# A rank-one memory layer in blocks of 32: block rows in a factored form, and their products placed behind the next block's pivots

## Chip, cores and metric

One Trainium2 chip (trn2), one core. The metric is the device time of one execution in microseconds (us), for the whole program.

## What is computed

A decoder of four layers over 64 sequences of 128 tokens with 128 channels. The change concerns the first operation of layer 0, a memory with a recursive least-squares state per sequence:

```
Q, K, V = x Wq + bq, x Wk + bk, x Wv + bv        # (64, 128, 128) each
A = eye(128); M = 0                              # per sequence
for t in range(128):
    s = sum(k * q)
    u = k / (norm(k) + 1e-6)
    Au = A @ u
    denom = 1 + sum(u * Au)
    A = A - outer(Au, Au) / denom
    z = Au / denom
    M = M + outer(v, s * z)
    o = M @ q
out = O @ Wo + bo
```

All vectors z (128 per sequence) and the dots s are computed first, by a memory phase; the decoder that follows (attention, experts and norms of all four layers) reads them from DRAM.

## The kernel before

The program has two parts, one behind the other: `memory_phase` and `decoder_phase`. All data is fp32. Each engine runs its own program; programs of several "threads" are merged by a string per engine in `MEMORY_ORDER`, one character for each step (up to a `yield`), executed in that order whatever is ready. A digit is a thread, w is the work that all share. SyncE issues all DMAs.

The memory phase handles 64 sequences as 16 quads of four; quad q belongs to thread q mod 4 (`THREADS = 4`), and each thread owns two PSUM banks, `Yb` and `Tb`. Stages:

- **Keys** (first loop of each `memory_quads_*`): TensorE projects queries and keys of a quad (L743), VectorE adds the bias (L839, L842), forms k times q (L848) and its sum, the dot s (L852), k times k (L855) and its sum (L859), GpSimd takes the root (L910), VectorE adds eps (L863), inverts (L867) and scales, giving u (L873). TensorE transposes u (L749), ScalarE evacuates it to `uT` (L807).
- **Block rows** for each block of 32 tokens (`BLK`, four blocks): for each quad y = U A, in both orientations (L765, L768), copied by ScalarE (L816) and VectorE (L881), then the Gram matrix g = y U^T of 32x32 per sequence (L775), copied to `g` (L886).
- **Trip of the small matrices**: SyncE stores g to DRAM (L995) and loads it with one sequence per partition into `E`, 64x32x64 (L999). VectorE adds 1 to the diagonal (L946) and does 31 pivots of an elimination, four instructions each (L953 to L963), for all sequences at once; then it writes the inverse factor and the same scaled by the inverse pivots into `xx` (L971, L974). SyncE stores xx (L1002) and loads it in eight DMAs as block-diagonal stationary operands `xs`, 128x128 for each quad (L1011).
- **Solve and update**: TensorE multiplies y by both factors (L791, L792) and gets the block's z (L793, copied by ScalarE over the keys in `uT`, L821). In the first three blocks, ScalarE copies W (L826), VectorE spreads the scaled product over four sequences with a mask (L894), one matmul of 512 columns forms the update (L798), and VectorE subtracts it from `A`, 128x128 for each sequence (L899). The next block's rows need the updated A.
- **End**: s and z are stored to DRAM (L1017, L1021), and the decoder's setup begins.

What sets the order around the change is thus a circle in each block: rows and Gram need A, the trip needs all 16 quads of g, the solve needs the trip, A needs the solve.

## Time and profile before

| | us |
|---|---|
| median of 3 runs | 6566.8 (6562.96 to 6573.8) |
| the profiled execution, its own time | 6575.45 |
| its span in the trace | 6573.4 |
| memory phase, to the end of the store of z | 655.72 |
| decoder with its setup | 5917.68 |

The trace is of one execution. Its stages are told apart by the DMAs of SyncE. PE is TensorE's matmuls, PEld its weight loads, DVE is VectorE, ACT ScalarE, POOL GpSimd, SPq SyncE's queue. One fp32 matmul of the program appears as two instructions. PEclk is the granted clock as a share of 2.4 GHz.

### The profile page before, as it was taken

What the parts mean: (1) busy time and instruction counts of PE and PEld (TensorE: products, weight loads), DVE (VectorE), ACT (ScalarE), POOL (GpSimd) and SP (SyncE); (2) the same over time, 40 slices, a digit from 0 to 9 for tenths busy, and PEclk for the clock granted to TensorE, in tenths of its full rate; (3) what the DMA queues carried; (4) which work ended last, traced back from release to release, by engine and by line L of the source; (5) the groups of instructions that cost most, each with busy time, mean ns of one, the idle gap of its engine ahead of it and who ended that gap; (6) DMA issues with size and microseconds to landing.
All of it is one profiled execution on the core that took longest, in us unless ns stands there. A gap on an engine that the chain in (4) does not pass through costs nothing.

```text
span 6573.4 us, 128828 instructions
## 1 busy us (share of the span) xinstructions
PE 5160.7 (79%) x54833; PEld 3769.1 (57%) x54833; DVE 3783.7 (58%) x9917; ACT 2358.7 (36%) x4452; POOL 512.8 (8%) x470
## 2 busy tenths in 40 slices
PE   5334477789897778888888888888778889878878
PEld 4223366556666556666656655666555566655656
DVE  6665256665555665655565565565655554566554
ACT  1000133443424344433443443433443433433442
POOL 1000100001100000100000001000100110000010
PEclk6666597999998989999888999999998989888989
DMA  1001210000021000001001001101000011100001
GB/s 31 10 17 38 75 52 27 1 1 27 21 80 38 16 1 17 28 28 56 27 27 34 27 2 34 38 23 52 9 27 16 20 36 50 38 16 16 14 1 49
DMA packets 144922, 184.39 MB, mean 28 GB/s; under 512 B 46202, under 2 KB 73826, under 8 KB 143714
## 3 DMA queue, kind: packets, MB, share of 16 engines
q1 hardware_dynamic: 144354, 176.17, 8.7%
q8 instruction: 436, 7.14, 0.5%
q14 instruction: 132, 1.08, 0.1%
HBM read 164.25 MB, written 11.57 MB: 27 GB/s over the span
## 4 chain that ended last, share of the span: by engine, by line
PE 59%; DVE 15%; ACT 8%; issue 5%; POOL 1%; DMA 1%; SPq 0%; POOLq 0%; DVEq 0%; ACTq 0%
PE g_bank L2515 7%; PE g_bank L2500 7%; PE g_bank L1426 5%; PE g_bank L1448 5%; PE g_bank L1398 5%; ACT g_keys_exps L1478 5%; DVE g_tops L1491 4%; PE g_bank L1459 2%; PE g_bank L1369 2%; PE g_bank L1773 2%; PE g_bank L1307 1%; PE g_bank L1787 1%; PE g_bank L2246 1%; PE g_bank L1411 1%; PE g_bank L2108 1%
## 5 line engine op out<-in xcount | busy, mean ns | idle before, releaser
L1491 DVE TENSOR_REDUCE g_tops<-g_bank 128x4 f32<-128x308 f32 (+1 forms) x1536 | 812.0, 574 | 535.6 <-PE g_bank L1398 532.4
L1478 ACT ACTIVATE g_keys_exps<-g_bank 77x512 f32<-77x512 f32 (+1 forms) x1536 | 802.5, 596 | 731.6 <-PE g_bank L1426 730.9
L1242 POOL TENSOR_TENSOR g_rstd<-g_rstd,minus_half 128x4 f32<-128x4 f32 x224 | 231.5, 1034 | 4560.8 <-DVE g_rstd L1225 4555.3
L1426 PE MATMUL g_bank<-g_qa,g_keys_exps 32*77 32x128 f32 (+1 forms) x12288 | 489.1, 302 | 112.5 <-DVE g_o L1511 59.8
L1426 PEld LDWEIGHTS g_bank<-g_qa,g_keys_exps 32*77 32x77 f32 (+1 forms) x12288 | 409.3, 183 | 227.9 <-DVE g_o L1511 83.5
L1398 PE MATMUL g_bank<-g_keys_exps,g_qa 32*128 32x154 f32 (+1 forms) x6144 | 415.4, 388 | 145.7 <-ACT g_keys_exps L1478 107.6
L1448 PE MATMUL g_bank<-g_keys_exps,g_v 77*32 77x128 f32 (+1 forms) x12288 | 455.8, 294 | 87.9 <-DVE g_tops L1491 74.9
L2515 PEld LDWEIGHTS g_bank<-L_places,g_keys_exps 128*128 128x128 f32 x4096 | 472.7, 192 | 51.7 <-issue 49.9
L2500 PE MATMUL g_bank<-g_xT,L_places 128*128 128x512 f32 x1024 | 496.0, 615 | 2.6 <-DMA L_places<-L_w_in 2.6
L2515 PE MATMUL g_bank<-L_places,g_keys_exps 128*128 128x128 f32 x4096 | 481.6, 276 | 7.8 <-DVE g_base L2545 7.7
L1448 PEld LDWEIGHTS g_bank<-g_keys_exps,g_v 77*32 77x32 f32 (+1 forms) x12288 | 343.1, 117 | 201.9 <-DVE g_tops L1491 146.9
L1472 ACT ACTIVATE g_oT_sc<-g_bank 128x512 f32<-128x512 f32 x384 | 228.5, 598 | 603.7 <-PE g_bank L1448 603.2
L1398 PEld LDWEIGHTS g_bank<-g_keys_exps,g_qa 32*128 32x128 f32 x6144 | 278.2, 203 | 260.0 <-ACT g_keys_exps L1478 146.5
L2526 ACT ACTIVATE g_keys_exps<-g_bank,weights_sb 128x512 f32<-128x512 f32 x256 | 175.6, 686 | 490.8 <-PE g_bank L2500 490.5
L2545 DVE SCALAR_TENSOR_TENSOR g_base<-g_bank,g_gates,g_base 128x128 f32<-128x128 f32 x512 | 152.6, 342 | 286.4 <-PE g_bank L2515 286.3
L1459 PE MATMUL g_bank<-consts_sb,g_oT_sc 128*128 128x128 f32 x1536 | 260.5, 295 | 52.7 <-ACT g_keys_exps L1478 25.2
L1494 DVE TENSOR_TENSOR g_qa<-g_qa,g_bank 128x256 f32<-128x256 f32 x384 | 159.7, 416 | 231.7 <-PE g_bank L1411 230.1
L2500 PEld LDWEIGHTS g_bank<-g_xT,L_places 128*128 128x128 f32 x1024 | 185.7, 196 | 178.0 <-issue 154.5
L791 PE MATMUL m_bank<-m_y,m_xs 128*128 128x128 f32 x128 | 29.4, 316 | 320.8 <-DMA m_xs<-xx_scratch 320.8
L2538 DVE TENSOR_SCALAR g_keys_exps<-g_bank,weights_sb 128x512 f32<-128x512 f32 x256 | 189.2, 745 | 146.2 <-PE g_bank L2500 146.1
L1251 ACT ACTIVATE g_x<-g_x,g_shift,g_rstd 128x128 f32<-128x128 f32 x384 | 176.8, 487 | 229.8 <-DVE g_shift L1228 229.2
L1459 PEld LDWEIGHTS g_bank<-consts_sb,g_oT_sc 128*128 128x128 f32 x1536 | 177.8, 148 | 136.2 <-issue 64.6
(360 smaller groups left out, 9170.3 us busy)
## 6 DMA issues: line engine op xcount, KB each, us to landing
L_places<-L_w_in SPq DMA_DIRECT2D x512, 256.0 KB, 2.8
m_xT<-xT_in SPq DMA_DIRECT2D x16, 256.0 KB, 2.7
z_scratch<-m_uT SPq DMA_DIRECT2D x1, 4096.0 KB, 11.1
g_oT_sc<-z_scratch SPq DMA_DIRECT2D x16, 256.0 KB, 2.9
g_xT<-xT_in SPq DMA_DIRECT2D x16, 256.0 KB, 3.5
g_o<-x_in SPq DMA_DIRECT2D x16, 256.0 KB, 4.0
out<-g_x SPq DMA_DIRECT2D x16, 256.0 KB, 2.3
weights_sb<-weights_in SPq DMA_DIRECT2D x1, 3021.0 KB, 9.9
```

What stands on the lines that cost most here:

```text
L1242: e.tensor_tensor(g.rstd[:, :], g.rstd[:, :], g.s["minus_half"], ALU.pow).then_inc(*b.gpsimd(st + " rstd"))
L1251: e.activation(out[:, n, :], src[:, n, :], ACT.Identity, bias=g.shift[:, n:n + 1], scale=g.rstd[:, n:n + 1]).then_inc(*b.scalar(f"{st} nor ...
L1398: ins = e.matmul(bank[r][:, 2 * nk * t:2 * nk * (t + 1)].rearrange("p (i k) -> p i k", i=2), g.qa[rows, t, n, :], g.km[rows, n, t, :, 0:nk ...
L1426: ins = e.matmul(bank[r][0:nk, u * T:(u + 1) * T], g.km[rows, n, t, i, 0:nk], g.qa[rows, t, n, :], start=not masked, stop=not masked or u ...
L1448: ins = e.matmul(b.bank[st][0][32 * u:32 * u + 32, r * T:(r + 1) * T], g.v[0:nk, n, 4 * r + u, :], g.p[0:nk, r, u, :], start=True, stop=True)
L1459: ins = e.transpose(b.bank[st][1][:, r * P:(r + 1) * P], outputs_of(g, n)[:, r, :], g.k["ident"])
L1472: e.activation(outputs_of(g, n - 1), seqs(bank[0][:, :]), ACT.Copy).then_inc(*b.scalar(f"{st} oT {n - 1}"))
L1478: e.activation(g.p[0:nk, r, :, :], bank[r][0:nk, :].rearrange("p (u q) -> p u q", u=4), ACT.Exp, scale=scale).then_inc(*b.scalar(f"{st} p ...
L1491: e.tensor_reduce(g.tops[:, :, first:first + 2], src, AX, ALU.max).then_inc(*b.vector(f"{st} top {n} {r}"))
L2500: e.matmul(bank[k % 3][:, :], weights.part(f"w1 {x}", c), g.xT, start=True, stop=True).then_inc(*b.tensor(f"f3 hidden {k}"))
L2515: ins = e.matmul(bank[3][:, n * D:(n + 1) * D], g.gated_hid[:, x % 2, c, n * T:(n + 1) * T], weights.part(f"w2 {x}", c), start=c == 0, sto ...
L2538: e.tensor_scalar(g.gated_hid[:, x % 2, k % HC, :], b.bank["ex"][k % 3][:, :], g.w["f3_b1"][:, k:k + 1], 0.0, ALU.add, ALU.max).then_inc(* ...
```

## The change

A is no longer formed or updated. With blocks before it solved, A = I minus a sum of terms, one per block, so a block's rows times the columns that are still needed are: U times [later keys | I], minus V_i times W_i for each earlier block i. `rows` holds for each quad (four sequences, 32 partitions each) those products with the keys of the later blocks (columns up to 128) and with I (128 more). W_i is the factor (now with the sign changed) times rows, V_i the scaled factor times the part over later keys.

- **Keys**: three threads. k times q moves to GpSimd, the squares to ScalarE with accumulation (the second product and the second sum leave VectorE). The first block's Gram matrix is U U^T, four small matmuls a quad into one bank `diag` (bank 6) for all quads, and one copy of 128x512 to g.
- **rest_tensor, rest_scalar**: one block's rows without the diagonal columns, and, for the block before, the remaining columns of W and V and its z. They have no VectorE part.
- **early_diagonal**: the part of the next block's Gram matrix that doesn't need the block's factors, accumulated in `diag`.
- **next_pairs, next_diagonal**: once the factors are loaded, W and V for the next block's 32 columns alone, in four chunks of four quads, and their product, added to `diag`. W is copied by ScalarE, V by VectorE.
- The last block has its solve alone; z is copied by ScalarE and VectorE in four pieces.
- The load of the mask is gone; xx gets the factor multiplied by -1. Elimination, DMAs of g, E, xx and xs are as before, with waits on one semaphore instead of four.

Cut to its core (the order strings, semaphores and the loops of the keys are left out but for what moves between engines):

```diff
-THREADS = 4
+THREADS = 3
...
+def keys_tensor_of(e, me, i):
...
+        e.wait_ge(me.uT_set[i], n + 1)
+        for j in range(4):
+            u = me.uT[:, 4 * q + j, cols_of(0)]
+            ins = e.matmul(me.diag[32 * j:32 * j + 32, q * BLK:(q + 1) * BLK], u, u, start=True, stop=True)
+        ins.then_inc(me.gram[i], 1)
+        yield
+def keys_scalar_of(e, me, i):
...
+            e.activation(me.squares[i][:, b, :], me.qk[i][:, b, D:2 * D], ACT.Square,
+                         accum_out=me.norm[:, 4 * q + b:4 * q + b + 1]).then_inc(me.squared[i], 1)
...
+def keys_gpsimd_of(e, me, i):
...
+        e.tensor_tensor(me.tmp[i][:, :, :], me.qk[i][:, :, D:2 * D], me.qk[i][:, :, 0:D], ALU.mult
+                        ).then_inc(me.multiplied[i], 1)
...
+def rest_tensor(e, me, blk):
+
+    at = (blk + 1) * BLK
+    own = cols_of(blk)
+    for q in range(me.nq):
+        done = blk * me.nq + q
+        W_bank, rows_bank = me.bank[q % 2 * 2], me.bank[q % 2 * 2 + 1]
+        if blk:
+            before = done - me.nq
+            e.wait_ge(me.rows_set, before + 1)
+            if before >= 2:
+                e.wait_ge(me.W_set, before - 1)
+                e.wait_ge(me.z_set, before - 1)
+                e.wait_ge(me.V_set, min(before - 1, (NBLK - 2) * me.nq))
+            x, scaled, rows = me.xs[:, q, 0, :], me.xs[:, q, 1, :], me.rows[:, q, :]
+            e.matmul(W_bank[:, 0:T + D - at], x, rows[:, at:T + D], start=True, stop=True)
+            if at < T:
+                e.matmul(W_bank[:, 256:256 + T - at], scaled, rows[:, at:T], start=True, stop=True)
+            e.matmul(W_bank[:, 384:512], rows[:, T:T + D], scaled, start=True, stop=True).then_inc(me.solved, 1)
+            yield
+            e.wait_ge(me.W_set, before + 1)
+            if at < T:
+                e.wait_ge(me.V_set, before + 1)
+        else:
+            for i in range(THREADS):
+                e.wait_ge(me.uT_set[i], len(quads_of(me, i)))
+        if done >= 2:
+            e.wait_ge(me.rows_set, done - 1)
+        for j in range(4):
+            lane, u = slice(32 * j, 32 * j + 32), me.uT[:, 4 * q + j, :]
+            if at < T:
+                e.matmul(rows_bank[lane, at:T], u[:, own], u[:, at:T], start=True, stop=False)
+            ins = e.matmul(rows_bank[lane, T:T + D], u[:, own], me.ident[:, :], start=at == T, stop=blk == 0)
+        for i in range(blk):
+            for j in range(4):
+                lane = slice(32 * j, 32 * j + 32)
+                ins = e.matmul(rows_bank[lane, at:T + D], me.V[lane, i, q, own.start - BLK:own.stop - BLK],
+                               me.W[lane, i, q, at - BLK:], start=False, stop=i == blk - 1)
+        ins.then_inc(me.rows_ready, 1)
+        yield
+
+def rest_scalar(e, me, blk):
...
+            e.wait_ge(me.solved, before + 1)
+            e.activation(me.W[:, blk - 1, q, at - BLK:], W_bank[:, 0:T + D - at], ACT.Copy).then_inc(me.W_set, 1)
+            yield
+            if at < T:
+                e.wait_ge(me.solved, before + 1)
+                e.activation(me.V[:, blk - 1, q, at - BLK:], W_bank[:, 256:256 + T - at], ACT.Copy).then_inc(me.V_set, 1)
+                yield
+            e.wait_ge(me.solved, before + 1)
+            e.activation(me.uT[:, 4 * q:4 * q + 4, cols_of(blk - 1)], four(W_bank[:, 384:512]), ACT.Copy
+                         ).then_inc(me.z_set, 1)
+            yield
+        e.wait_ge(me.rows_ready, done + 1)
+        e.activation(me.rows[:, q, at:], rows_bank[:, at:T + D], ACT.Copy).then_inc(me.rows_set, 1)
+        yield
...
+def early_diagonal(e, me, blk):
+
+    own = cols_of(blk + 1)
+    e.wait_ge(me.g_set, blk + 1)
+    for q in range(me.nq):
+        at = slice(q * BLK, (q + 1) * BLK)
+        for j in range(4):
+            u = me.uT[:, 4 * q + j, own]
+            e.matmul(me.diag[32 * j:32 * j + 32, at], u, u, start=q == 0, stop=False)
+        for i in range(blk):
+            for j in range(4):
+                lane = slice(32 * j, 32 * j + 32)
+                e.matmul(me.diag[lane, at], me.V[lane, i, q, cols_of(blk)], me.W[lane, i, q, cols_of(blk)],
+                         start=False, stop=False)
+        yield
+
...
+PAIR_BANKS = ((4, 5), (7, 0), (1, 2), (3, 4))
+
+
+def pairs_in(me, c, k):
+    return me.bank[PAIR_BANKS[c][k]][:, 0:4 * BLK].rearrange("p (q m) -> p q m", q=4)
...
+def next_pairs(e, me, blk, c):
+
+    at = (blk + 1) * BLK
+    if c == 1:
+        e.wait_ge(me.rows_set, (blk + 1) * me.nq)
+        if blk:
+            e.wait_ge(me.W_set, blk * me.nq)
+            e.wait_ge(me.V_set, blk * me.nq)
+            e.wait_ge(me.z_set, blk * me.nq)
+    elif c == 3:
+        e.wait_ge(me.next_W, 4 * blk + 1)
+    for q in range(4 * c, 4 * c + 4):
+        e.wait_ge(me.rows_set, blk * me.nq + q + 1)
+        out = slice(q % 4 * BLK, (q % 4 + 1) * BLK)
+        for k in range(2):
+            ins = e.matmul(me.bank[PAIR_BANKS[c][k]][:, out], me.xs[:, q, k, :], me.rows[:, q, at:at + BLK],
+                           start=True, stop=True)
+    ins.then_inc(me.pair_ready, 1)
+    yield
+
+
+def next_diagonal(e, me, blk, c):
+
+    part = cols_of(blk)
+    e.wait_ge(me.next_W, 4 * blk + c + 1)
+    e.wait_ge(me.next_V, 4 * blk + c + 1)
+    for q in range(4 * c, 4 * c + 4):
+        at = slice(q * BLK, (q + 1) * BLK)
+        for j in range(4):
+            lane = slice(32 * j, 32 * j + 32)
+            ins = e.matmul(me.diag[lane, at], me.V[lane, blk, q, part], me.W[lane, blk, q, part], start=False,
+                           stop=q == me.nq - 1)
+    ins.then_inc(me.diag_ready, 1)
+    yield
...
+def memory_tensor(e, me):
+
+    chunks = me.nq // 4
+    for blk in range(NBLK):
+        yield from rest_tensor(e, me, blk)
+        if blk < NBLK - 1:
+            yield from early_diagonal(e, me, blk)
+        e.wait_ge(me.xs_loaded, 128 * (blk + 1))
+        if blk < NBLK - 1:
+            if blk:
+                e.wait_ge(me.next_W, 4 * blk)
+                e.wait_ge(me.next_V, 4 * blk)
+            yield from next_pairs(e, me, blk, 0)
+            for c in range(1, chunks):
+                yield from next_pairs(e, me, blk, c)
+                yield from next_diagonal(e, me, blk, c - 1)
+            yield from next_diagonal(e, me, blk, chunks - 1)
+    for q in range(me.nq):
+        e.wait_ge(me.rows_set, NBLK * me.nq)
+        e.wait_ge(me.W_set, (NBLK - 1) * me.nq)
+        e.wait_ge(me.z_set, (NBLK - 1) * me.nq)
+        e.matmul(me.bank[q // 4][:, (q % 4) * P:(q % 4 + 1) * P], me.rows[:, q, T:T + D], me.xs[:, q, 1, :],
...
@@ memory_vector, in the loop over the blocks, behind the clears of E
+        if blk:
...
+            for c in range(me.nq // 4):
+                e.wait_ge(me.pair_ready, 4 * blk - 4 + c + 1)
+                e.tensor_copy(me.V[:, blk - 1, 4 * c:4 * c + 4, cols_of(blk - 1)], pairs_in(me, c, 1)).then_inc(me.next_V, 1)
+                yield
+            e.wait_ge(me.diag_ready, 4 * blk)
+            e.wait_ge(me.g_stored, 16 * blk)
+        else:
...
+        e.tensor_copy(me.g[:, :, :], me.diag[:, :].rearrange("p (q c) -> p q c", c=BLK)).then_inc(me.g_set, 1)
@@ memory_vector, behind the elimination
-        e.tensor_copy(me.xx[:, :, 0:BLK], inv_T).then_inc(me.xx_set, 1)
+        e.tensor_scalar(me.xx[:, :, 0:BLK], inv_T, -1.0, None, ALU.mult).then_inc(me.xx_set, 1)
```

How it moves instructions, at two places. First TensorE, from the solve of the first block on. `m_xs` are the loaded factors, `m_y` and `m_rows` the block's rows, `m_z` and `m_w` the operands of the update. Before, where the factors have just come:

```order
L791 MATMUL m_bank<-m_y,m_xs 128x128
L792 MATMUL m_bank<-m_y,m_xs 128x128
L793 MATMUL m_bank<-m_xs,m_y 128x128
...
L798 MATMUL m_bank<-m_z,m_w 128x512 x3
...
L765 MATMUL m_bank<-m_A,m_uT 32x128 x4
L768 MATMUL m_bank<-m_uT,m_A 128x32 x4
L775 MATMUL m_bank<-m_uT,m_yT 32x32 x4
```

And now, from the last rows of block 0 to the first products of block 1's rest:

```order
L867 MATMUL m_bank<-m_ident,m_uT 32x128
L909 MATMUL m_bank<-m_uT 32x32 x64
L941 MATMUL m_bank<-m_rows,m_xs 128x32 x16
L956 MATMUL m_bank<-m_W,m_V 32x32 x16
L941 MATMUL m_bank<-m_rows,m_xs 128x32 x8
...
L956 MATMUL m_bank<-m_W,m_V 32x32 x32
L850 MATMUL m_bank<-m_rows,m_xs 128x192
L852 MATMUL m_bank<-m_rows,m_xs 128x64
L853 MATMUL m_bank<-m_xs,m_rows 128x128
```

The wait for the factors stands between the rows L909 and the first L941; all that a quad had between factors and g is now 32 columns wide, and the full-width solve (L850 to L853) stands behind the last diagonal product. Second VectorE, between one block's factors and the next block's pivots. `m_E` holds the small matrices. Before:

```order
L974 TENSOR_TENSOR m_xx<-m_E,m_rd 64x32x32
L940 MEMSET m_E 64x32x32
L894 TENSOR_TENSOR m_z<-m_bank,m_group_mask 128x512
L943 MEMSET m_E 64x32
...
L899 TENSOR_TENSOR m_A<-m_A,m_bank 128x512 x3
...
L881 COPY m_yT<-m_bank 128x128
...
L886 COPY m_g<-m_bank 128x32
L946 TENSOR_SCALAR m_E<-m_E 64x32
```

Now:

```order
L1072 TENSOR_TENSOR m_xx<-m_E,m_rd 64x32x32
L1026 MEMSET m_E 64x32x32
L1029 MEMSET m_E 64x32
L1034 COPY m_V<-m_bank 128x4x32 x4
L1041 COPY m_g<-m_bank 128x512
L1044 TENSOR_SCALAR m_E<-m_E 64x32
```

Thirty-nine rows of spreads, subtractions and small copies have become five copies.

## Rows read from the trace of the kernel before

**Rows 1.** The page, busy us of each engine, share of the span, instructions.
```profile
PE 5160.7 (79%) x54833; PEld 3769.1 (57%) x54833; DVE 3783.7 (58%) x9917; ACT 2358.7 (36%) x4452; POOL 512.8 (8%) x470
```

**Rows 2.** Stages: window, length, busy of PE, PEld, DVE, ACT, POOL, PEclk, DMA, GB/s.
```profile
0.00:132.20 132.20, 95.63 (x576) 73.18 (x576) 78.85 (x178) 23.70 (x49) 22.19 (x22) 0.72 0.12 35
132.20:212.05 79.85, 0.00 (x0) 0.00 (x1) 57.49 (x128) 0.00 (x0) 0.00 (x0) 0.50 0.12 20
212.05:270.97 58.92, 57.19 (x512) 42.38 (x512) 29.67 (x66) 11.56 (x48) 0.00 (x0) 0.85 0.01 1
351.22:412.16 60.94, 59.25 (x512) 43.37 (x512) 29.67 (x66) 11.56 (x48) 0.00 (x0) 0.81 0.00 1
491.64:550.68 59.04, 57.26 (x512) 42.43 (x512) 29.66 (x66) 11.56 (x48) 0.00 (x0) 0.85 0.01 1
630.50:644.20 13.70, 13.29 (x96) 13.10 (x96) 0.00 (x0) 4.43 (x16) 0.00 (x0) 0.83 0.00 0
644.20:655.72 11.52, 0.00 (x0) 0.00 (x0) 0.00 (x0) 0.00 (x0) 0.01 (x1) 0.70 0.85 364
655.72:6573.40 5917.68, 4878.11 (x52625) 3554.62 (x52625) 3385.90 (x9029) 2295.86 (x4243) 490.58 (x448) 0.91 0.09 29
...
20.00:40.00 20.00, 13.48 (x44) 10.23 (x44) 16.85 (x34) 1.84 (x4) 5.04 (x5) 0.74 0.14 39
...
215.00:232.00 17.00, 17.00 (x92) 11.46 (x95) 14.96 (x22) 5.34 (x24) 0.00 (x0) 0.99 0.00 1
```

**Rows 3.** Timeline of SyncE's queue, first trip: start us, us, DMA issued.
```profile
132.20 0.39 SPq L995 DMA_DIRECT2D g_scratch<-m_g  x1
...
201.63 0.50 SPq L1002 DMA_DIRECT2D xx_scratch<-m_xx  x1
```

**Rows 4.** Instruction groups of the first 800 us: count, busy us, mean ns, idle before.
```profile
L910 POOL TENSOR_TENSOR m_norm<-m_norm,m_half 128x4 f32<-128x4 f32 x16 | 18.4, 1152 | 84.9 <-DVE m_norm L859 84.9
...
L839 DVE TENSOR_TENSOR m_qk<-m_bank,m_qkb 128x512 f32<-128x512 f32 x16 | 11.0, 686 | 13.8 <-PE m_bank L743 13.8
...
L873 DVE TENSOR_TENSOR m_u<-m_qk,m_norm 128x512 f32<-128x512 f32 x16 | 10.9, 681 | 0.0
...
L852 DVE TENSOR_REDUCE m_s_all<-m_tmp 128x4 f32<-128x512 f32 x16 | 10.8, 675 | 0.0
```

**Rows 5.** Instruction groups: reciprocal and eps, a ScalarE copy and accumulator reading, GpSimd.
```profile
L867 DVE RECIPROCAL m_norm<-m_norm 128x4 f32<-128x4 f32 x16 | 2.7, 168 | 0.0
L863 DVE TENSOR_SCALAR m_norm<-m_norm 128x4 f32<-128x4 f32 x16 | 2.6, 163 | 4.7 <-POOL m_norm L910 4.7
...
L821 ACT ACTIVATE m_uT<-m_bank 128x128 f32<-128x128 f32 x64 | 17.7, 277 | 378.7 <-PE m_bank L793 378.7
...
L2142 ACT ACTIVATION_READ_ACCUMULATOR g_keys_exps<-g_keys_exps,g_small 128x1 f32 x64 | 12.2, 190 | 0.0
...
L1293 POOL TENSOR_TENSOR g_base<-g_x,rows_sb 128x512 f32<-128x512 f32 x48 | 58.7, 1224 | 73.2 <-ACT g_x L1251 72.1 <-DVE g_keys_exps L1324 1.1
```

**Rows 6.** Timeline of TensorE: start us, us, line, operands, count.
```profile
213.50 0.63 PE L791 MATMUL m_bank<-m_y,m_xs 128*128 128x128 f32 x2
...
214.78 0.63 PE L791 MATMUL m_bank<-m_y,m_xs 128*128 128x128 f32 x2
...
218.27 0.38 PE L791 MATMUL m_bank<-m_y,m_xs 128*128 128x128 f32 x2
...
218.93 0.39 PE L791 MATMUL m_bank<-m_y,m_xs 128*128 128x128 f32 x2
...
231.93 0.42 PE L765 MATMUL m_bank<-m_A,m_uT 128*32 128x128 f32 x8
232.28 1.08 PE L768 MATMUL m_bank<-m_uT,m_A 128*128 128x32 f32 x8
233.20 1.10 PE L798 MATMUL m_bank<-m_z,m_w 128*128 128x512 f32 x2
...
756.47 2.01 PE L1426 MATMUL g_bank<-g_qa,g_keys_exps 32*77 32x128 f32 x32 [0.51 <-DVE g_qa L1494]
```

More of the change, by code:

```diff
@@ L730, in memory_quads_sync @@
         yield
-def memory_quads_tensor(e, me, i):
-    Yb, Tb = me.bank[2 * i], me.bank[2 * i + 1]
-    for q in quads_of(me, i):
-        n = q // THREADS
-        e.wait_ge(me.weights_loaded, 64)
+def keys_tensor_of(e, me, i):
+    first, last = me.bank[2 * i], me.bank[2 * i + 1]
+    for n, q in enumerate(quads_of(me, i)):
+        e.wait_ge(me.weights_loaded, 48)
         e.wait_ge(me.x_loaded[i], 16 * (n + 1))
@@ L741, in memory_quads_tensor @@
             e.wait_ge(me.uT_set[i], n)
+            e.wait_ge(me.last_biased[i], n)
         for b in range(4):
-            ins = e.matmul((Yb, Tb)[b // 2][:, (b % 2) * 256:(b % 2) * 256 + 256], me.xT[i][:, b, :], me.qkw[:, :],
-                           start=True, stop=True)
+            out = (first, last)[b // 2][:, (b % 2) * 256:(b % 2) * 256 + 256]
+            ins = e.matmul(out, me.xT[i][:, b, :], me.qkw[:, :], start=True, stop=True)
         ins.then_inc(me.projected[i], 1)
@@ L836, in memory_quads_vector, with keys_vector_of @@
+def keys_vector_of(e, me, i):
+    first, last = me.bank[2 * i], me.bank[2 * i + 1]
+    for n, q in enumerate(quads_of(me, i)):
         r = slice(4 * q, 4 * q + 4)
-        kk, qq = me.qk[i][:, :, D:2 * D], me.qk[i][:, :, 0:D]
         e.wait_ge(me.projected[i], n + 1)
-        e.tensor_tensor(me.qk[i][:, 0:2, :], Yb[:, :].rearrange("p (b c) -> p b c", b=2), over(me.qkb[:, :], 1, 2),
-                        ALU.add).then_inc(me.biased[i], 1)
+        if n:
+            e.wait_ge(me.u_set[i], n)
+            e.wait_ge(me.multiplied[i], n)
+            e.wait_ge(me.squared[i], 4 * n)
+        e.tensor_tensor(me.qk[i][:, 0:2, :], first[:, :].rearrange("p (b c) -> p b c", b=2), over(me.qkb[:, :], 1, 2),
+                        ALU.add).then_inc(me.first_biased[i], 1)
@@ new lines, in last_result @@
+def last_result(e, me, q):
+    e.wait_ge(me.solved, (NBLK - 1) * me.nq + q + 4)
+    return me.uT[:, 4 * q:4 * q + 16, cols_of(NBLK - 1)], me.bank[q // 4][:, :].rearrange("p (b t) -> p b t", b=16)
+def memory_scalar(e, me):
+    for blk in range(NBLK):
+        yield from rest_scalar(e, me, blk)
+        if blk < NBLK - 1:
+            for c in range(me.nq // 4):
+                e.wait_ge(me.pair_ready, 4 * blk + c + 1)
+                e.activation(me.W[:, blk, 4 * c:4 * c + 4, cols_of(blk)], pairs_in(me, c, 0), ACT.Copy).then_inc(me.next_W, 1)
+                yield
+    for q in (0, 8):
+        out, src = last_result(e, me, q)
+        e.activation(out, src, ACT.Copy).then_inc(me.z_set, 1)
```

301 lines of the change are left out of this document (105 added, 196 removed).

## Prediction

> **What bounds the kernel now.** I read the page's busy shares first, then the span cut into stages, then the DMA queue's own timeline, then the instruction groups of each stage. The busy shares say only that TensorE is the busiest engine over the whole span [rows 1]; the change touches the memory phase alone, so the table by stage is what counts [rows 2]. It shows a phase of 655.72 us with a strict alternation. First 132.20 us for keys and the first block's rows. Then, four times, a stretch of about 80 us in which TensorE and ScalarE do nothing and VectorE is busy 57.5 us: that is one trip of the small matrices, from the store of g over the elimination to the loaded factors (132.20 to 212.05 the first time; the others lie between the rows: 270.97 to 351.22, 412.16 to 491.64, 550.68 to 630.50). Behind the first three trips stand 58.92, 60.94 and 59.04 us in which TensorE is busy 97% of the time: solve, update of A, next rows, next Gram matrix. Behind the fourth, 13.70 us of solving and 11.52 us of storing z. The other 5917.68 us are the decoder. So the phase is a serial sum: pivots on VectorE wait for products on TensorE and the reverse, and nothing of the two overlaps. Inside a trip, SyncE stores g at 132.20 and can issue the store of the factors only at 201.63 [rows 3].
>
> **The change, part by part.** The sum goes stage by stage.
>
> *Trips.* Store of g, load of E, 31 pivots, store and loads of the factors: same instructions, one copy turned into a multiplication by -1 of the same 64x1024 elements. I cost it at nothing; the four trips stay 79.85 + 80.25 + 79.48 + 79.82 = 319.40 us [rows 2].
>
> *Keys.* Before, a quad of sequences costs VectorE two additions of the bias, two products, two sums, an addition of eps, a reciprocal and the scaling, and the first block's rows and Gram matrix stand behind them. Now VectorE keeps two additions (the second like the first), one sum, eps, reciprocal and scaling: 0.69 + 0.69 + 0.68 + 0.16 + 0.17 + 0.68 = 3.07 us a quad, 49 us for 16 [rows 4, 5]. One product goes to GpSimd, at 1.22 us as an addition of 128x512 elements in the decoder, beside the root at 1.15: 2.4 us a quad [rows 4, 5]. The squares go to ScalarE: four activations of 128 elements, each with the reading of its accumulator, 4 x (0.28 + 0.19) = 1.9 us a quad [rows 5]. The first block's rows leave this stage entirely, since its Gram matrix is now the product of keys with themselves: four small matmuls a quad instead of twelve. VectorE is again the busiest of four fairly even engines, with each quad a chain through all of them and three instead of four quads under way. Lower bound: 49 us of VectorE, 8 us until its first operand (an allowance: the addition of the bias waits 13.8 us for TensorE in all, most of it at the start) and 4 us of tail (transposes, evacuation, Gram, one 128x512 copy to g at 0.69): 61 us. Upper bound: 94 us, below as a rival. Before, in a steady piece of this stage, VectorE was busy 16.85 of 20 us, 84% [rows 2]; with more hops between engines and fewer quads under way I take 78%: 49 / 0.78 + 8 + 3 = 74 us. Gain 58.2 us.
>
> *Boundaries.* What stands between loaded factors and the next g shrinks to the next block's 32 columns. TensorE first does 4 quads x 2 matmuls of 32 columns against a 128x128 stationary operand. In the trace a matmul in fp32 is two instructions; the clock granted in the trips is the low one (0.50, 1.2 GHz) [rows 2], and after such a trip six instructions take 1.28 us (213 ns each), later 0.66 (110 ns each) [rows 6]. A 32-column one against a full stationary operand takes as long, 0.92 us for eight [rows 6]. So chunk 0 costs 16 x 0.213 = 3.4 us, chunks 1 to 3 cost 16 x 0.110 each, 5.3. Each chunk's diagonal is 16 matmuls, 32 instructions, of a 32x32 tile with 32 columns. No row shows this tile. Nearest rows: eight instructions of 128 columns in four column tiles in 0.35 us, 44 ns each, a quarter of that for 32 columns is 11 ns; and 32 instructions of 128 columns in row tiles in 2.01 us, 63 ns each [rows 6]. I take 30 ns, in between, since fewer columns leave issuing as the limit: 4 x 32 x 0.03 = 4 us. Evacuation of the last chunk and two hand-overs 0.5, copy to g 0.8. Sum 14.0 us (11.4 to 23, the upper end being the low clock throughout with 63 ns). V's copies run on VectorE behind two clears of E (1.0 us), inside chunk 0. Three boundaries: 178.90 - 42.0 = gain 136.9 us. The updates of A, with the spreads on VectorE and the 128x512 products on TensorE, vanish altogether.
>
> *The rest*, now behind the pivots. Cover: 80.6 us from the finished diagonal to the loaded factors; no solve may end later than the store of the factors, 69.4 us after that of g [rows 3], or the loads wait. In block 1 a quad needs 384 columns of solving (0.67 us), two evacuations with hand-overs (0.75), 16 instructions for keys and identity, 8 for V times W. With column tiles at 44 ns per 128 columns: 2.5 us a quad; one after another at 110: 4.1. So 40 to 66 us. Block 2, with two V times W terms: 2.6 to 4.6, so 41 to 73 us, plus its early diagonal, 384 instructions at 11 to 63 ns: 4 to 24, middle 11. Block 3: 38 to 72. ScalarE's four evacuations a quad come to about 1.2 us and fit. In the middle I get 65 us for the worst block against 80.6, so the cost is nothing; it is that cover, the pivots, that hides it.
>
> The hardest price here is V times W. Four lanes of 32 rows write four lanes of one bank; the rows of before with row tiles write to four different banks (bank[r] in the decoder's attention) and so don't show this case. The Trainium skill, "TensorEngine Tiling (Array Packing)", section Gotcha 1, says that different row tiles can't access one PSUM bank at the same time. By it the lanes would run one after another, the upper figures above; no row before shows whether they do. The sum would then be the first rival's.
>
> *End.* Sixteen matmuls (32 instructions) remain behind the fourth trip: 16 x 0.213 + 16 x 0.110 = 5.2, a copy of 128x512 at 0.69, hand-overs 0.2: 6.1 instead of 13.70. Gain 7.6 us. The store of z, 11.52 us, stays, and so does the decoder, whose instructions and order are the same.
>
> **Sum.** 74.0 + 319.4 + 42.0 + 6.1 + 11.5 + 5917.7 = 6370.7 us of span against 6573.4: 202.7 less. The profiled execution's own time is 6575.45, so 6372.7 for it. That execution lies 8.65 us over the median of the three timed runs, 6566.8; against the median I predict 6364 us.
>
> **Rivals.**
>
> 1. *Lanes one after another, at the full clock.* Block 2 needs 73 + 24 = 97 us against 80.6, and block 1 66 + 16 = 82. Overrun 17 us: 6381. For it: no row shows concurrency of this tile inside one bank. Against: even then the cover nearly holds. I count it inside the forecast, as a shade of it.
>
> 2. *Keys not faster through GpSimd.* VectorE's scaling and GpSimd's product would get in each other's way. For it: both engines are to work on SBUF through all of this stage, and the two are busy 49 and 38 us of it. If each quad pays one GpSimd product, 1.22 us [rows 5], more on the chain's busiest engine, 16 x 1.22 = 20 us: keys end at 94, 6384 us. The Trainium skill, "SBUF — State Buffer", section Who interferes with whom, has such a rule: a VectorE instruction with two SBUF inputs and a GpSimd instruction that reads SBUF block each other for the whole instruction. No row here isolates that.
>
> 3. *The rest outgrows its cover in part*: lanes serial and the low clock for about half of it, because the hand-overs leave TensorE with gaps. Overruns of 10 to 40 us a block: 6400 to 6500. For it: the granted clock in the boundary stages is 0.81 to 0.85 even with TensorE 97% busy [rows 2]. Against: in the first such stage, from 3 us after its start, the grant is 0.99 over 17 us, with waits between groups [rows 2].
>
> 4. *Slower than before.* The same mechanism in full: all of the rest at 1.2 GHz and one after another. Block 1: 2 x (0.67 + 1.34 + 1.34) + 0.75 = 7.45 us a quad, 119, plus 32 for its early diagonal; block 2: 8.4 a quad, 135, plus 48; block 3: 8.6, 138. Beyond 80.6 us each that is 70 + 102 + 57 = 229, more than the 203 gained: 6593 us. It decides from about 148 us of rest a block, 9.3 us a quad where I expect 3.4. That the change doesn't do what it says, products behind pivots, is this case too. Against: the grants of 0.81 and 0.85 leave at most a third of the busy stages before at the low level.
>
> **How the numbers follow.** Forecast, with shade 1: 0.76. Rival 2: 0.12. Rival 3: 0.08. Rival 4: 0.04. The best ends together (keys 61, boundaries 11.4, end 5, runs 5 us lower) give 6337, the worst (keys 94, boundaries 23, rest 17 over) 6428, but not all fall together; 6335 to 6415 leaves rivals 3 and 4 and a little more out. The measurement can tell about 0.2%, 13 us. Rival 4 ends 0.4% slower; between it and rival 3 lies a sliver within 0.2%. Faster 0.95, same 0.01, slower 0.04.
>
> **What would show it.** The first store of g at about 74 us, the next at 74 + 94 = 168, then 262 and 356; the store of z issued near 442 and the decoder starting near 453; TensorE busy inside the trips and idle again before each set of factors lands; VectorE's wait between the clears of E and the copy to g near 13 us. The prediction is wrong where TensorE's idle time before the loaded factors is gone (rivals 3, 4), where the store of the factors waits for a solve, or where the decoder, 5917.7 us, is no longer the same.

## The result, and the profile after

The changed kernel takes 6389.4 us (median of 4 runs, 6375.5 to 6391.4), the kernel before, beside it, 6564.9 us (4 runs, 6558.3 to 6573.8): a ratio of 0.973, 95% interval 0.971 to 0.975. Faster, as forecast, and inside the range; but 25 us above the predicted 6364. The profiled execution took 6388.6 us with a span of 6386.5.

The table by stage of the changed kernel (columns as in [rows 2]) answers to [rows 2] line by line: keys, then a trip and a boundary three times, the fourth trip, the last solve, the store of z, the decoder.

```profile
0.00:80.34 80.34, 54.44 (x376) 40.63 (x380) 50.44 (x99) 32.45 (x147) 43.44 (x38) 0.88 0.19 57
80.34:160.40 80.06, 8.90 (x337) 6.68 (x330) 57.51 (x128) 5.01 (x14) 0.00 (x0) 0.59 0.12 20
160.40:177.61 17.21, 17.21 (x195) 16.82 (x196) 2.86 (x7) 1.11 (x4) 0.00 (x0) 0.50 0.00 1
177.61:257.40 79.79, 42.93 (x735) 28.94 (x733) 57.52 (x128) 15.14 (x64) 0.00 (x0) 0.74 0.13 21
257.40:274.71 17.31, 17.20 (x196) 16.82 (x196) 2.85 (x7) 1.11 (x4) 0.00 (x0) 0.50 0.00 1
274.71:354.80 80.09, 43.86 (x992) 31.24 (x990) 57.55 (x128) 13.85 (x64) 0.00 (x0) 0.78 0.13 22
354.80:371.91 17.11, 17.11 (x196) 16.73 (x196) 2.86 (x7) 1.11 (x4) 0.00 (x0) 0.50 0.01 1
371.91:451.60 79.69, 34.44 (x574) 22.73 (x573) 57.52 (x128) 11.57 (x48) 0.00 (x0) 0.69 0.13 21
451.60:458.89 7.29, 6.40 (x32) 6.21 (x32) 1.38 (x2) 1.19 (x2) 0.00 (x0) 0.62 0.00 0
458.89:470.41 11.52, 0.00 (x0) 0.00 (x0) 0.00 (x0) 0.00 (x0) 0.01 (x1) 0.57 0.85 364
470.41:6386.50 5916.09, 4879.18 (x52625) 3556.64 (x52625) 3387.94 (x9029) 2298.16 (x4243) 490.81 (x448) 0.91 0.09 29
```

Two things have changed shape. The trips are as long as before (80.06, 79.79, 80.09, 79.69 us), but TensorE, which had nothing to do in them, is now busy 34 to 44 us in each after the first: the rest stands behind the pivots. And the boundaries have shrunk from about 59 us to 17.2, in which TensorE is busy all the time at a granted clock of 0.50. The phase went from 655.7 to 470.4 us.

TensorE's timeline through the first boundary, and through one quad of block 2's rest (start us, us, instruction, count):

```profile
160.40 7.03 PE L941 MATMUL m_bank<-m_rows,m_xs 128*128 128x32 f32 x32 [66.62 <-DMA m_xs<-xx_scratch]
167.36 0.65 PE L956 MATMUL m_bank<-m_W,m_V 32*32 32x32 f32 x32
167.94 3.62 PE L941 MATMUL m_bank<-m_rows,m_xs 128*128 128x32 f32 x16
171.50 0.65 PE L956 MATMUL m_bank<-m_W,m_V 32*32 32x32 f32 x32
172.08 3.62 PE L941 MATMUL m_bank<-m_rows,m_xs 128*128 128x32 f32 x16
175.63 1.20 PE L956 MATMUL m_bank<-m_W,m_V 32*32 32x32 f32 x64
...
280.34 0.26 PE L866 MATMUL m_bank<-m_uT 128*32 128x32 f32 x5 [0.53 <-ACT m_W L886]
...
280.78 0.75 PE L871 MATMUL m_bank<-m_W,m_V 32*32 32x160 f32 x16
281.46 0.54 PE L850 MATMUL m_bank<-m_rows,m_xs 128*128 128x160 f32 x2
281.83 0.30 PE L852 MATMUL m_bank<-m_rows,m_xs 128*128 128x32 f32 x2
```

Read from start to start, chunks 0 and 1 of the pairs take 6.96 us for 32 instructions, 218 ns each, and the later chunks 3.56 us for 16, 222 ns: no chunk is faster than the first. The diagonal's 32x32 tiles take 18 ns each (0.58 us for 32). A warm quad of the rest takes 2.63 us, of which V times W takes 0.68 us for 16 instructions in lanes, 42 ns each, where two full-width ones of the same 160 columns (L850) take 185 ns each.

The keys, as instruction groups up to the first store of g: GpSimd's product, VectorE's scaling and VectorE's addition of eps. Below them rows of the timelines of GpSimd and VectorE around 46 and 69 us.

```profile
L826 POOL TENSOR_TENSOR m_tmp<-m_qk 128x512 f32<-128x512 f32 x16 | 23.4, 1461 | 30.1 <-DVE m_qk L792 13.2 <-issue 9.1 <-DVE m_qk L796 7.7
...
L813 DVE TENSOR_TENSOR m_u<-m_qk,m_norm 128x512 f32<-128x512 f32 x16 | 12.4, 777 | 0.3
...
L803 DVE TENSOR_SCALAR m_norm<-m_norm 128x4 f32<-128x4 f32 x16 | 4.8, 298 | 2.8 <-POOL m_norm L831 2.8
...
45.95 1.27 POOL L826 TENSOR_TENSOR m_tmp<-m_qk 128x512 f32<-128x512 f32 x1
...
46.01 1.23 DVE L803 TENSOR_SCALAR m_norm<-m_norm 128x4 f32<-128x4 f32 x1 [0.28 <-POOL m_norm L831]
...
69.25 1.81 POOL L826 TENSOR_TENSOR m_tmp<-m_qk 128x512 f32<-128x512 f32 x1 [2.94 <-DVE m_qk L792]
...
69.24 0.69 DVE L813 TENSOR_TENSOR m_u<-m_qk,m_norm 128x512 f32<-128x512 f32 x1
```

An addition of eps to four numbers a partition, 163 ns before [rows 5], lasts 1.23 us here and ends with GpSimd's product, which began just ahead of it. Of its 16 executions 14 take 0.16 or 0.17 us and two 1.22 and 1.23, of the scaling's 14 take 0.68 or 0.69 and two 1.18 and 1.63; of GpSimd's products nine take 1.26 or 1.27 and seven 1.59 to 1.81, against 1.22 in the decoder [rows 5]. The long ones go in pairs: each of the four long instructions of VectorE starts while a product of GpSimd is under way, and each of the seven long products starts 0.01 to 0.22 us behind a scaling (69.25 behind 69.24).

### The profile page after: what moved, and what is told of

It reads as the page before. It is cut to its first block, busy times and chain, and to the rows that moved or that the text cites. A ratio compares the mean times of both kernels' runs of the same rounds, so it can differ in the third digit from the quotient of the medians.

```text
span 6386.5 us, 131296 instructions
## 1 busy us (share of the span) xinstructions
PE 5121.7 (80%) x56241; PEld 3743.4 (59%) x56241; DVE 3678.4 (58%) x9663; ACT 2380.7 (37%) x4594; POOL 534.3 (8%) x486
## 4 chain that ended last, share of the span: by engine, by line
PE 60%; DVE 16%; ACT 9%; issue 5%; POOL 1%; DMA 1%; SPq 0%; POOLq 0%; DVEq 0%; ACTq 0%
PE g_bank L2616 7%; PE g_bank L2601 7%; PE g_bank L1527 6%; PE g_bank L1549 5%; PE g_bank L1499 5%; ACT g_keys_exps L1579 5%; DVE g_tops L1592 4%; PE g_bank L1560 2%; PE g_bank L1470 2%; PE g_bank L1874 2%; PE g_bank L1888 2%; PE g_bank L1408 2%; PE g_bank L2347 1%; PE g_bank L2209 1%; PE g_bank L1512 1%
## 5 line engine op out<-in xcount | busy, mean ns | idle before, releaser
L1549 PEld LDWEIGHTS g_bank<-g_keys_exps,g_v 77*32 77x32 f32 (+1 forms) x12288 | 342.2, 117 | 202.0 <-DVE g_tops L1592 147.8
L1512 PE MATMUL g_bank<-consts_sb,g_tops 128*128 128x128 f32 x768 | 169.5, 305 | 102.9 <-DVE g_tops L1592 99.7
```

The source lines that it names most:

```text
L1512: ins = e.transpose(bank[2][:, t * T:(t + 1) * T], g.tops[:, t, :], g.k["ident"])
L1549: ins = e.matmul(b.bank[st][0][32 * u:32 * u + 32, r * T:(r + 1) * T], g.v[0:nk, n, 4 * r + u, :], g.p[0:nk, r, u, :], start=True, stop=True)
```

## Experiments

Ten kernels, each an edit of the changed one. "Phase" is the time until the decoder's first DMA, 470.4 us in the changed kernel; a "circle" is the time from one store of g to the next. Where no ratio is given, the kernel was executed once, and its trace is read stage by stage.

**Placement or form?** `rest_in_front` puts all of a block's rest back in front of its g.

```diff
@@ memory_vector, before the copy to g
+        e.wait_ge(me.rows_set, (blk + 1) * me.nq)
         e.tensor_copy(me.g[:, :, :], ...).then_inc(me.g_set, 1)
```

> VectorE's copy to g waits until the rest of the block before is done, so the products stand in front of the pivots again, in the factored form. Theory A (the placement behind the pivots earns most of the gain): the stretch between the store of g and the loaded factors stays 80 us, and each boundary grows by the rest of its block, in the changed kernel's trace 13 us for the first block (in the keys' tail), 46 and 44 us for the next two, and 41 us before the last g's pivots; the memory phase goes from 470 to about 600 to 615 us. Theory B (the factored form itself, fewer and smaller products, earns most): the phase stays under 540 us.

Measured: 6538.3 us, phase 618.2. Windows: keys up to the first store of g, then the stretch before each of the next three, counted from some 0.3 us after TensorE's first use of the factors (171.00 for 170.74).

```profile
0.00:91.02 91.02, 63.08 (x576) 46.66 (x576) 50.41 (x99) 37.46 (x161) 43.48 (x38) 0.89 0.18 51
171.00:237.78 66.78, 56.24 (x672) 42.13 (x672) 2.81 (x7) 16.24 (x68) 0.00 (x0) 0.71 0.01 1
317.90:384.56 66.66, 57.00 (x800) 43.67 (x800) 2.80 (x7) 14.96 (x68) 0.00 (x0) 0.74 0.01 2
464.80:519.59 54.79, 47.73 (x768) 37.21 (x768) 2.79 (x7) 12.67 (x52) 0.00 (x0) 0.81 0.01 2
```

The phase is 3 us above the 600 to 615 that I had expected, far from the 540 of the other theory. With the rest in front, the boundaries are 67.0, 66.9 and 55.1 us, together 10.1 longer than before (58.9, 60.9, 59.0). Of the phase's gain of 185.3 us, 147.8 go with the placement. The 37.5 left are the 41.2 of the keys (91.0 instead of 132.2) and 6.5 from the last store of g to the store of z (87.0 instead of 93.5), less those 10.1. So the factored form, cut in two as here, saves nothing in the boundaries by itself. It is worth having because it leaves something that can be moved.

**Is the cover real?** `rest_thrice` issues each product V times W of the rest three times in a row (that term counts triple in the result); `rest_thrice_alternating` issues as many instructions, with the repetition outermost, so that neighbours work on different lanes.

```diff
@@ rest_tensor, rest_thrice
+                for again in range(3):
+                    ins = e.matmul(rows_bank[lane, at:T + D], ...)
@@ rest_tensor, rest_thrice_alternating
+        for again in range(3):
+            for i in range(blk):
+                for j in range(4):
```

> Each V times W product of the rest is issued three times, so the term that is subtracted counts triple in the rows of blocks 1 to 3. Theory A (the rest is hidden with room to spare, so its price on the span is nothing): it adds 2 x 0.5 to 2 x 1.0 us a quad, 16 to 32 us a block, the rest then takes up to 76 us of the 80, and the store of z is issued within 3 us of the changed kernel's 458.9. Theory B (the rest is already at the edge of its cover, or slows the pivots' traffic): the boundaries or the trips grow by 10 us or more a block.

> The term V times W of the rest counts triple, with the same number of instructions as in rest_thrice, but the loop of the repetitions stands outside those over earlier blocks and lanes, so that neighbouring instructions work on different tiles. Theory A (what made rest_thrice 164 us longer in the phase is the same tile several times in a row, which makes lanes wait for each other and keeps the granted clock low): 42 ns an instruction at the full clock and 100 at the low one, so 13 to 26 us more in block 1, 21 to 51 in block 2, 25 to 60 in block 3, against slack of 20 us and more; memory phase 470 to 520 us, and V times W well under the 170 ns an instruction of rest_thrice. Theory B (the amount of work alone, the clock low through the rest): 600 us and more, 170 ns an instruction as before.

Measured: in a row 6563.6 us, phase 634.2; alternating 6373.5 us, phase 470.8, which is 0.4 us more than without any extra work. First the windows of the three rests of `rest_thrice`, then of `rest_thrice_alternating`:

```profile
178.79:295.00 116.21, 106.91 (x767) 63.76 (x765) 57.60 (x128) 15.12 (x64) 0.00 (x0) 0.50 0.09 14
319.74:455.00 135.26, 126.82 (x1119) 82.93 (x1117) 57.55 (x128) 13.54 (x63) 0.00 (x0) 0.50 0.08 13
482.44:614.00 131.56, 125.69 (x1333) 94.40 (x1335) 57.57 (x128) 11.28 (x47) 0.00 (x0) 0.50 0.08 13
```

```profile
178.60:256.00 77.40, 51.20 (x991) 35.48 (x989) 57.49 (x128) 15.13 (x64) 0.00 (x0) 0.83 0.11 20
275.31:353.00 77.69, 59.81 (x1503) 46.01 (x1501) 57.55 (x128) 13.83 (x64) 0.00 (x0) 0.92 0.12 20
372.73:450.00 77.27, 52.71 (x1342) 42.43 (x1341) 57.48 (x128) 11.56 (x48) 0.00 (x0) 0.88 0.11 20
```

And the same 24 instructions of block 1, a cold quad of each kernel (`rest_thrice`, then alternating, whose second row is a warm quad):

```profile
181.21 4.07 PE L872 MATMUL m_bank<-m_W,m_V 32*32 32x192 f32 x24
```

```profile
181.01 2.14 PE L872 MATMUL m_bank<-m_W,m_V 32*32 32x192 f32 x24
...
185.61 1.18 PE L872 MATMUL m_bank<-m_W,m_V 32*32 32x192 f32 x24
```

With the same tile three times running, an instruction takes 166 ns (3.99 us from start to start for 24), alternating 87 ns at the low clock and 46 at the full one. In `rest_thrice` the granted clock stayed at 0.50 through 107 to 127 us of busy TensorE a block, and the loads of xs, which wait for the last solve, came 36 us late in the first overrun: 40.5 us behind the store of xx, where the changed kernel has 4.2.

```profile
248.27 0.47 SPq L1101 DMA_DIRECT2D xx_scratch<-m_xx  x1
288.79 4.03 SPq L1109 DMA_DIRECT2D m_xs<-xx_scratch  x8
```

For `rest_thrice` I had expected 16 to 32 us a block; measured, the circles of blocks 1 to 3 are 44, 65 and 53 us longer. That is rivals 3 and 4 made real, with nearly all of the gain gone (6563.6 against 6571.5 for the kernel before on that chip, one execution each). But it isn't the amount of work: the alternating kernel does the same amount and ends on time. Its expectation of 470 to 520 us allowed for more than it needed. So the cover of the changed kernel holds with room for twice the V times W on top, as long as neighbouring instructions go to different tiles. The clock stayed low in the kernel in which TensorE was busier (92% of the first row's 116 us, against 84% of the 57.4 us from 178.6 to 236.0, through which the alternating rest runs at a grant of 0.95); why is open.

**The first diagonal, early or late.** `early_late` moves the early diagonal behind the loaded factors.

```diff
@@ memory_tensor
-            yield from early_diagonal(e, me, blk)
...
+            yield from early_diagonal(e, me, blk)
             yield from next_pairs(e, me, blk, 0)
```

> The part of the next Gram matrix that needs no factors is computed after the factors are loaded instead of during the pivots. Theory A (it is small but costs its full time once it stands on the path, and at the low clock): boundaries grow from 17.2 us by about 2, 5 and 8 us for the three blocks (128, 256 and 384 instructions at 18 ns or so), the phase by about 15 us. Theory B (more TensorE work ahead of the 32-column matmuls raises the granted clock, which pays it back): the boundaries stay within 2 us of 17.2.

Measured: 6408.7 us, phase 489.7, 19.3 more, where 15 had been expected. g is stored at 81.11, 180.01, 285.21 and 392.32, so the circles grow from 97.3, 97.1, 97.2 us to 98.9, 105.2 and 107.1. In front of the second and third boundary stand 8.4 and about 10 us of small products, all at the low clock: from 365.0 to 375.0 us, and on through the third boundary, TensorE is busy without a gap at a granted clock of 0.50. In the changed kernel the cover hides these products as well.

**The keys.** `product_on_vector` moves k times q back from GpSimd to VectorE, in front of its sum.

```diff
@@ keys_gpsimd_of
-        e.tensor_tensor(me.tmp[i][:, :, :], ..., ALU.mult).then_inc(me.multiplied[i], 1)
@@ keys_vector_of, before tensor_reduce
...
+        e.tensor_tensor(me.tmp[i][:, :, :], ..., ALU.mult).then_inc(me.multiplied[i], 1)
+        e.wait_ge(me.multiplied[i], n + 1)
```

> The product of k and q goes back from GpSimd to VectorE, in the place of its sum. Theory A (VectorE's work bounds the stage of the keys): VectorE gets 16 x 0.68 = 11 us more and the first store of g goes from 80.3 to about 88 to 92 us. Theory B (the stage is bound by the chain through GpSimd and the conflict of GpSimd's product with VectorE's scaling, which takes 0.78 us where it took 0.68 before): the scaling falls back to 0.68, the root waits for nothing, and the first store of g comes at 80 us or earlier.

Measured: 6363.5 us, first store of g at 74.63 instead of 80.34, phase 462.7.

```profile
0.00:74.63 74.63, 52.06 (x376) 39.30 (x380) 57.05 (x115) 32.22 (x147) 21.70 (x22) 0.90 0.21 62
...
40.00:60.00 20.00, 14.30 (x104) 10.53 (x104) 19.02 (x39) 10.84 (x52) 5.67 (x6) 0.98 0.20 60
```

The product costs VectorE 11.0 us (16 x 685 ns). Its busy time rises by only 6.6, from 50.4 to 57.1, since the scalings are back at 688 ns and no addition of eps is over 0.17 us; and in a steady piece it is busy 19.02 of 20 us. So moving this product to GpSimd had made the stage 5.7 us longer, not shorter. One execution shows it, but the other kernels bear it out: with the product on GpSimd the first g is stored between 80.3 and 81.4 us in seven kernels whose keys are the same, with it on VectorE at 74.6, 75.1 and 76.5 in three.

**The boundary.** `pairs_in_lanes` multiplies the pairs of 32 columns lane by lane: a quad's stationary operand is block-diagonal, and its zero blocks are left out. `warm_before` instead gives TensorE 22 matmuls of 256 columns, read by nobody, from the store of the factors on; `lanes_and_warm` has both.

```diff
@@ next_pairs, in lanes
+            for j in range(4):
+                lane = slice(32 * j, 32 * j + 32)
+                ins = e.matmul(me.bank[PAIR_BANKS[c][k]][lane, out], me.xs[lane, q, k, lane],
+                               me.rows[lane, q, at:at + BLK], start=True, stop=True)
@@ memory_tensor, warm: before the wait for xs_loaded
...
+        e.wait_ge(me.xx_stored, 16 * (blk + 1))
+        for _ in range(22):
+            e.matmul(me.bank[7][:, 0:256], me.ident[:, :], me.qkw[:, :], start=True, stop=True)
```

> The products of the factors with the next 32 columns use the four 32x32 blocks on the diagonal of each stationary operand, eight small matmuls a quad instead of two with a full 128x128 operand. Theory A (a boundary's 17.2 us are 64 instructions' worth of full weight loads at 213 ns, 13.6 us): a 32x32 tile costs 18 ns an instruction, as the diagonal products do in the changed kernel, so 16 quads take 16 x 16 x 0.018 = 4.6 us, each boundary goes from 17.2 to about 8 to 9 us, and the phase loses 25 us. Theory B (row tiles that write one PSUM bank run one after another): 16 x 16 instructions at 60 ns or more, 15 us, and the boundary stays at 17 us or grows.

> 22 matmuls of 256 columns, whose result nobody reads, run on TensorE between the store of the factors and their arrival, so that the clock is up when the factors land. Theory A (the boundary ran at the low level because TensorE had idled before it): with the grant at 1.00 the 16 quads of full weight loads take 110 ns an instruction, 7 us, and each boundary goes from 17.2 to 9 to 10 us; the last solve from 7.3 to about 5; phase 24 us shorter. Theory B (the matmuls of 32 columns themselves let the grant fall or keep it low, whatever ran before): the grant is back at 0.50 within the boundary, which stays above 13 us.

> Both together: small tiles and the clock raised before the factors land. If the weight loads were the price and the clock the other half of it, a boundary comes to 6 to 7 us; if VectorE's clears of E and the evacuations in four chunks with their hand-overs bound it once the matmuls are short, it stays at 7 to 8.5 us and the warm-up adds nothing over the tiles alone.

Measured, four runs each: 6357.6 us in lanes (ratio to the kernel before 0.9678, 0.9661 to 0.9694; phase 450.3), 6400.0 with the warm-up (0.9734, 0.9719 to 0.9749; phase 477.1), 6358.3 with both (0.9679, 0.9665 to 0.9694; phase 469.4). First TensorE's timeline in the boundary of `pairs_in_lanes`, then of `warm_before`, then the latter's windows.

```profile
160.58 1.93 PE L943 MATMUL m_bank<-m_rows,m_xs 32*32 32x32 f32 x128 [66.72 <-DMA m_xs<-xx_scratch]
162.31 0.63 PE L958 MATMUL m_bank<-m_W,m_V 32*32 32x32 f32 x32
162.73 1.06 PE L943 MATMUL m_bank<-m_rows,m_xs 32*32 32x32 f32 x64
163.59 0.52 PE L958 MATMUL m_bank<-m_W,m_V 32*32 32x32 f32 x24
165.47 0.26 PE L958 MATMUL m_bank<-m_W,m_V 32*32 32x32 f32 x8 [1.36 <-issue]
...
169.33 0.37 PE L958 MATMUL m_bank<-m_W,m_V 32*32 32x32 f32 x10 [2.12 <-issue]
```

```profile
154.51 11.15 PE L974 MATMUL m_bank<-m_qkw,m_ident 128*128 128x256 f32 x44 [60.25 <-DMA xx_scratch<-m_xx]
165.50 3.65 PE L941 MATMUL m_bank<-m_rows,m_xs 128*128 128x32 f32 x32
...
172.22 3.62 PE L941 MATMUL m_bank<-m_rows,m_xs 128*128 128x32 f32 x16
```

```profile
160.00:168.00 8.00, 8.00 (x51) 7.34 (x49) 1.29 (x3) 0.28 (x1) 0.00 (x0) 1.00 0.00 0
168.00:172.00 4.00, 4.00 (x86) 3.85 (x88) 0.54 (x2) 0.53 (x2) 0.00 (x0) 0.88 0.02 4
172.00:177.00 5.00, 5.00 (x105) 4.81 (x93) 0.34 (x2) 0.31 (x2) 0.00 (x0) 0.50 0.00 0
```

Lanes: four times as many instructions, yet 13.5 ns each (1.73 us for 128) against 218, and a first boundary of 9.9 us instead of 17.2, where 8 to 9 had been expected. The warm-up does what it should at first, 32 pair instructions in 3.58 us, 112 ns each, the price I had forecast, and the next 16 in 2.17; but the grant is back at 0.50 before the last chunk, which again takes 222 ns an instruction. The filler also ran to 165.50, 5 us past the landing of the factors (taken as in the changed kernel, 10.5 us after the store of xx), and took back what it had given, 4.8 us in the pairs. With both, the filler ran to 166.82, some 5.5 us past the landing, and the next g was stored another 9.7 us after that, where lanes alone take 9.9 from the landing; for this kernel I had expected at most 8.5 us from the landing on, and hadn't counted the overrun. A filler that ends with the landing wasn't run on the wide form of the pairs.

**Together.** `product_and_pairs` has lanes and the product on VectorE; `product_pairs_short_warm` also half the filler, 11 matmuls.

> Both single improvements together: the products of keys and queries back on VectorE, and the next block's 32 columns of W and V multiplied lane by lane in 32x32 tiles (the blocks of a quad's stationary operand off the diagonal are zero and are left out). Theory A (the two gains are at different places and add): first store of g near 74.6 us, boundaries near 10 us each, store of z issued near 470.4 - 11.5 - 5.7 - 20.1 = 433, end of the memory phase near 444.6; the whole kernel near 6357.6 - 5.7 = 6352 us, a ratio to the kernel before of about 0.967. Theory B (VectorE's extra work moves the end of the keys of some quads behind others, and part of the gain is lost to later waits): phase 448 to 451.

> As product_and_pairs, and 11 matmuls of 256 columns, read by nobody, on TensorE from the end of the store of the factors: by the 11.2 us of 22 of them they last about 6 us, so that they end as the factors land. Theory A (the clock is worth something in boundaries of small tiles and in the last solve, and the longer filler only overran): boundaries 8 to 9 us, last stretch near 5 instead of 7.3 us, phase 3 to 7 us shorter than product_and_pairs, near 439. Theory B (boundaries of small tiles are limited by the supply of instructions, not by the clock): boundaries within 1 us of those of product_and_pairs, and only the last stretch is up to 2.5 us shorter; phase 442 to 445.

Measured, five and four runs: 6360.9 us (0.9683, 0.9667 to 0.9700) and 6353.0 us (0.9676, 0.9657 to 0.9694). The phases are 442.3 and 446.3 us. The first is 28.1 less than the changed kernel's; 25.8 had been expected of the sum, so the gains add in the phase. The whole kernel came 9 us above the 6352 expected. The phase with the short filler, 446.3, lies above both of its theories (439, and 442 to 445). This filler saves nothing: it takes 6.9 to 8.0 us where I had counted on 6, ends 1 to 2 us after the factors (taken to land 10.4 and 10.1 us after the store of xx, as in `product_and_pairs`), and pairs and diagonals then take as long as without it (9.6 us in both). Of the 4.0 us that its phase is longer, 1.4 lie in the keys, ahead of the first filler. In the last stretch it wins 2.0 us in the solve and loses them by its own overrun:

```profile
422.56 7.90 PE L976 MATMUL m_bank<-m_qkw,m_ident 128*128 128x256 f32 x22 [34.25 <-DMA xx_scratch<-m_xx]
430.29 3.73 PE L991 MATMUL m_bank<-m_xs,m_rows 128*128 128x128 f32 x32
```

All four kernels with lanes beat the changed one (their intervals end at 0.9700 or below, its own begins at 0.9709), but the measurement does not rank them. `pairs_in_lanes` has 8 us more of phase than `product_and_pairs`, and its time is no longer. The spans show why: the decoder, with the same instructions in every kernel, took 5902.4 us in the profiled execution of `pairs_in_lanes`, 5921.6 in that of `product_and_pairs`, 5898.9 in `product_on_vector`, 5916.1 in the changed kernel; over all twelve kernels, one execution each, 5896.8 to 5927.2. A gain of 8 us in the phase can be read only in the phase.

## Why the prediction was right, and where it was off

Term by term, predicted and measured, in us of the profiled execution:

| term | predicted | measured | off by |
|---|---|---|---|
| keys, to the first store of g | 74.0 | 80.3 | +6.3 |
| four trips | 319.4 | 319.6 | +0.2 |
| three boundaries | 42.0 | 51.6 | +9.6 |
| last solve | 6.1 | 7.3 | +1.2 |
| store of z | 11.5 | 11.5 | 0 |
| decoder | 5917.7 | 5916.1 | -1.6 |
| span | 6370.7 | 6386.5 | +15.8 |

The other 9.6 us of the 25 are the step from the profiled execution to the median. I took off 8.65 us because that execution of the kernel before lay so far above its median; the one of the changed kernel lies 0.8 us below its own. The offset belonged to an execution, not to the kernel.

- **Boundaries: the mis-sized term, +9.6.** The step "chunks 1 to 3 cost 16 x 0.110 each" failed. It took from [rows 6] that TensorE's clock rises some 3 us after the factors, as it did in the solves of 128 columns. In the new boundary the grant is 0.50 to its end: 10.6 us for the three chunks instead of 5.3, +5.3 a boundary, and +0.1 in chunk 0. `warm_before` shows that a start at the full clock would have helped with a part only, since the grant falls back during these instructions with TensorE busy all the time. The diagonals went the other way, 18 ns an instruction for the 30 taken between 11 and 63, and the hand-overs cost nearly nothing: -1.7 and -0.5. 5.3 + 0.1 - 1.7 - 0.5 = 3.2 a boundary. The upper bound of 23 us had the low clock in it; the point value should have had it.
- **Keys: +6.3.** The step "VectorE 78% busy" failed. I had applied it to the stage without its 11 us of start and tail; there the 49 us of work are 71% of what was left (69.3), and in two steady pieces, 20 to 40 and 40 to 60 us, VectorE is busy 71 and 76%. (The sum has 3 us of tail where its lower bound has 4, so 1 us of the miss may be that.) What rival 2 is about, the product's move to GpSimd, accounts for most of it: `product_on_vector` puts the net price at 5.7, where I gave 0.12 to an all-or-nothing price of 20 us. The Trainium skill, "SBUF — State Buffer", section Who interferes with whom, says that GpSimd and a VectorE instruction with two SBUF inputs lock each other out of a shared port. The trace agrees for the scaling (777 against 681 ns), with each long instruction paired with one of the other engine, and an instruction with one tensor input, the eps of 1.23 us, was held in the same way. But 14 of 16 of each are undisturbed. Against `product_on_vector`, VectorE has 11.0 us of work less, 4.4 us of busy time come back, mostly as longer instructions, and its idle time is 12.3 us more (29.9 against 17.6), of which it waits 10.6 us for GpSimd's products. Some of these are the longer ones, so how much is interference and how much the extra hand-over in each quad's chain, no run separates.
- **The rest behind the pivots: right, and the cost was nothing.** Expected 2.5 to 4.1 us a quad; measured 4.1 cold and 2.6 warm. In block 2 it is done at 328, early diagonal included, 54 us after the boundary, for which 65 was the middle; TensorE then waits 26.4 us for the factors. Tripling V times W, alternating, moves the phase by 0.4 us: the slack is real.
- **Lanes in one bank (rival 1): not serial.** 42 ns an instruction in V times W where full-width ones take 185. The Trainium skill, "TensorEngine Tiling (Array Packing)", Gotcha 1, says that row tiles can't access one PSUM bank at the same time. Four row tiles that write to four different lanes of one bank show no such cost here; the same tile three times in a row does, a factor of 1.9 at the low clock (166 against 87 ns). Which of bank, row group or column group makes neighbours wait wasn't tried apart.
- **Rivals 3 and 4** need V times W both tripled and ordered badly, as `rest_thrice` shows; then they come true as described, with the low clock through the whole rest and the loads of xs waiting for the solves.
- **Last solve: +1.2.** The 32 instructions took 6.4 us, 200 ns each in the mean, where I had half of them at 110.
- **What I used as signs** came out in kind: the next g 97.3 us after the first instead of 94, TensorE idle 27.7, 26.4 and 39.5 us before the second to fourth factors, VectorE's waits in the first boundary 14.0 us instead of 13, the decoder unchanged. The times are late by the terms above: first g at 80.3 instead of 74, store of z at 458.9 instead of 442.

## What to carry to other kernels

A product that a serial chain waits for can be split into the few columns that the chain needs and a rest placed behind the chain's next step. What it earns is the placement (148 of 185 us here), and the reformulation only makes it possible. What remained in front here was short and made of small instructions; it ran at the low clock, so it had to be priced there, and reshaped for its size: leaving out the zero blocks gave 20 us of phase that no warm-up gave. Moving work to GpSimd from a busy VectorE has to be measured by the stage, not by the instructions that are gone.
